# A decoder's expert routing: row numbers by rank replaced by block ids summed on TensorE

## The chip, the cores and the metric

The kernel runs on one core of one Trainium2 chip. Its time is the device time of one execution in microseconds (us). Engines are written PE (TensorE), ACT (ScalarE), DVE (VectorE), POOL (GpSimd) and SP (SyncE, which here only issues DMAs). Each has its own in-order queue of instructions, and they wait for one another through semaphores.

## The reference, cut to what matters

Two decoder layers in float32 on x of shape (16, 64, 128), that is 1024 tokens of width 128, or 8 tiles of 128 tokens. Layer 0: causal self attention with rotary positions (16 heads of width 8), cross attention to `ctx_1024`, then a mixture of 8 experts; layer 1: self attention with 16 heads of width 64, cross attention, then a feed-forward layer with ternary weights. After each of the six a residual sum and a layer norm. The part that the change is about:

```
logits = x_flat @ gate_w.T                      # (1024, 8)
top_v, top_i = top_k(logits, 2)
probs = softmax(top_v)
combine = einsum('tk,tke->et', probs, one_hot(top_i, 8))
for wg, wu, wd, we in experts:                  # wg, wu (512, 128), wd (128, 512)
    hidden = silu(x_flat @ wg.T) * (x_flat @ wu.T)
    acc = acc + we[:, None] * (hidden @ wd.T)
```

## The kernel before, in words

The attention and feed-forward layers run as two streams of tiles, `pre` (self0, cross0: 16 tiles) and `post` (wide, cross1, ternary: 24 tiles). A stream is software pipelined: in step j each engine works for several tiles at different stages (`stream_pe`, `stream_act`, `stream_dve`, `stream_pool`), and hooks (`pre_pe` and its like, lines 1933 to 1982) put other work between. Behind the `pre` stream, the order of what is left of tiles S[5] to S[7] (the last three tiles of cross0), of routing and of the weights' transposes is written out by hand, one list per engine: `drain_pe`, `drain_act`, `drain_dve`, `drain_pool` (lines 1997 to 2097). An engine works through its list strictly in order.

Routing (class `Routed`). The 8 token tiles are taken in groups (`GROUPS`, line 1427: tiles 0-1, 2-3, 4-5, 6, 7). For each group:
- `logits_pe`, `logits_act`: 128x8 logits per tile, copied from PSUM.
- `choose` (DVE): the two best experts by Max8 and its index search, one-hot rows OH, their sum `chosen`, and a running sum `before`.
- `rank_pe`: for each token and expert, the number of earlier tokens that chose it, as products of `chosen` and `before` with constant matrices.
- `place_read`, `place` (DVE): this rank plus the expert's base (1024 rows for each) picked by OH, giving a row number `pos`.
- `scatter` (POOL): two indirect DMAs per tile write the tile's rows into the DRAM tensor `routed` at `pos`, 16 in all. SP has filled `routed` (4544 KB) with zeros before (line 2169).

When all groups are done, `map_dve` works out with 12 small steps which expert each of the 23 blocks of 128 rows belongs to and at which row it starts. `rows_sp` loads 23 starts into SP's registers and loads the blocks of `routed` directly into XG; it stores each block's result back in place. PE and POOL load the 23 expert numbers into registers.

The 24 expert matrices (gate, up, down of 8 experts) come by DMA in natural layout and are turned in place by PE: 4 transposes into one bank and a copy back each (`weights_pe`, `weights_copy`). 17 of them stand in `drain_pe`, the rest at the head of `Routed.pe`; ACT copies 20 and DVE 4 (`DVE_WEIGHTS`).

The block loop (`Routed.pe`, `act`, `dve`, `pool`, lines 1762 to 1866), for block n: transpose of the block's rows (`block_pe`, `block_act`), gate product, Silu on ACT, up product, product of both on DVE (`mul_dve`), down product, copy to YS on DVE (`out_dve`), store. POOL brings the gate and up weights of the block's expert into a ring of three (`bring_pool`, line 1708: a 128x1024 copy from an address in a register), since PE reads them from a fixed place. Between blocks 6 and 12 DVE and POOL also prepare the ternary weights and separate WQKV (three 128x1024 copies, line 1853).

Behind the last block POOL gathers each token's two result rows by `pos` with 16 indirect DMAs (line 1871), DVE weighs and adds them (`combine`), normalises (`rsqrt` on POOL, `apply` on DVE), and the `post` stream starts.

## Time and profile before

| what | us |
|---|---|
| median of 3 runs | 361.52 (359.88 to 361.73) |
| profiled execution, its own time | 356.69 |
| span of the profiled execution | 354.9 |
| PE busy | 315.3 (89% of the span) |
| DVE busy | 226.5 |
| POOL busy | 192.2 |
| ACT busy | 185.1 |

All times of the trace count from the start of the span. A line number such as L1720 is one of the kernel before. A busy PE is not a PE at its peak: its matrix instructions are pipelined and overlap. "Granted clock" is the share of full speed that the chip allowed PE in a stretch: 1.00 is 2.4 GHz, 0.50 is 1.2 GHz. Spans on POOL are rough.

### The profile page before, as it was taken

Reading aid. Unit: us, or ns where it says so; the run is one execution under the profiler, and the core shown is the slowest. Engines: PE = TensorE matmul, PEld = TensorE weight load, DVE = VectorE, ACT = ScalarE, POOL = GpSimd, SP = SyncE. Lnnn points to the kernel's source line nnn. Section 1 sums busy time; section 2 is a strip of 40 time slices with the busy share of each in tenths; the row PEclk is TensorE's granted clock in tenths of the full one; section 3 lists DMA queues with packets and bytes.
Section 4 is the critical chain, followed back from the end, with each engine's and each line's share of the span. In section 5 each row is a group of like instructions: output and inputs, shape, how many; then the busy total and the mean of one; then the engine's idle time right before and its main releaser. Section 6 shows DMA issues by size and latency. Waiting matters only on the chain.

```text
span 354.9 us, 10572 instructions
## 1 busy us (share of the span) xinstructions
PE 315.3 (89%) x4062; PEld 261.5 (74%) x4062; DVE 226.5 (64%) x529; ACT 185.1 (52%) x402; POOL 192.2 (54%) x282
## 2 busy tenths in 40 slices
PE   2769999997896799999995999999999987999993
PEld 2547787886786699999984966688677665887663
DVE  1398988889657334653336475665566675897685
ACT  2276787887466332332223367454435436788641
POOL 2676867885775555534306884231123355486785
PEclk9999999999769999999998799999999999999998
DMA  6899989000111111121011110000000000000001
GB/s 186 233 311 281 293 270 317 12 3 3 39 37 46 53 47 45 46 57 52 22 31 30 46 40 9 2 2 2 2 2 1 4 1 2 2 4 3 3 22 40
DMA packets 35979, 23.04 MB, mean 65 GB/s; under 512 B 4160, under 2 KB 33882, under 8 KB 35802
## 3 DMA queue, kind: packets, MB, share of 16 engines
q1 hardware_dynamic: 34618, 19.64, 19.1%
q0 software_dynamic: 1024, 2.10, 1.9%
q8 instruction: 34, 0.56, 0.7%
q10 hardware_dynamic: 288, 0.62, 0.5%
q14 instruction: 15, 0.12, 0.1%
HBM read 14.60 MB, written 7.73 MB: 63 GB/s over the span
## 4 chain that ended last, share of the span: by engine, by line
PE 70%; DVE 10%; POOL 6%; issue 6%; DMA 3%; ACT 2%; SPq 1%; POOLq 0%; ACTq 0%; DVEq 0%
PE banks L924 9%; PE banks L934 8%; PE banks L1751 6%; PE banks L1720 6%; PE banks L1728 6%; PE banks L463 6%; PE banks L636 5%; PE banks L968 4%; PE banks L609 3%; PE banks L562 2%; PE banks L948 2%; PE banks L1125 2%; PE banks L1493 2%; PE banks L588 2%; PE banks L571 1%
## 5 line engine op out<-in xcount | busy, mean ns | idle before, releaser
L472 ACT ACTIVATE PT<-banks 128x512 f32<-128x512 f32 x64 | 34.8, 597 | 22.2 <-PE banks L463 21.6
L974 ACT ACTIVATE U<-banks 128x512 f32<-128x512 f32 x47 | 28.1, 597 | 28.6 <-PE banks L924 15.3
L1708 POOL COPY U<-WALL 128x1024 f32 x23 | 23.8, 1041 | 33.1 <-PE banks L1728 29.4
L335 POOL TENSOR_SCALAR ve<-mv 128x1 f32<-128x1 f32 x40 | 9.0, 225 | 54.5 <-DVE mv L330 53.8
L1743 DVE TENSOR_TENSOR PT<-banks,PR 128x512 f32<-128x512 f32 x23 | 15.9, 691 | 35.0 <-PE banks L1728 29.0
L451 ACT ACTIVATE PR<-PR 128x1024 f32<-128x1024 f32 x32 | 33.8, 1057 | 6.8 <-DVE PR L445 6.6
L463 PE MATMUL banks<-cst,PR 128*128 128x128 f32 x256 | 34.1, 276 | 2.7 <-issue 0.8
L924 PE MATMUL banks<-XT,WQKV 128*128 128x128 f32 x256 | 33.0, 291 | 0.8 <-ACT XT L1915 0.8
L924 PEld LDWEIGHTS banks<-XT,WQKV 128*128 128x128 f32 x256 | 31.4, 204 | 1.6 <-ACT XT L1915 1.2
L463 PEld LDWEIGHTS banks<-cst,PR 128*128 128x128 f32 x256 | 28.0, 141 | 5.8 <-issue 3.5
L428 DVE TENSOR_REDUCE mx<-banks 128x16 f32<-128x1024 f32 x24 | 29.3, 1220 | 3.8 <-PE banks L620 2.5
L445 DVE TENSOR_TENSOR PR<-banks,mx 128x1024 f32<-128x1024 f32 x24 | 29.4, 1224 | 0.8
L934 PE MATMUL banks<-WALL,XT 128*64 128x512 f32 x128 | 29.2, 598 | 0.0
L780 POOL TENSOR_TENSOR RK<-KQ,cst 128x512 f32<-128x512 f32 x24 | 24.9, 1039 | 4.3 <-DVE KQ L745 2.8
L636 PE MATMUL banks<-VB,PT 128*64 128x18 f32 x768 | 26.3, 212 | 0.0
L1003 POOL TENSOR_TENSOR PR<-PR,rs 128x1024 f32<-128x1024 f32 x8 | 15.2, 1901 | 20.2 <-DVE rs L1013 20.0
L636 PEld LDWEIGHTS banks<-VB,PT 128*64 128x64 f32 x768 | 25.0, 140 | 0.5 <-issue 0.2
L1751 PE MATMUL banks<-WALL,PT 128*128 x184 | 24.4, 276 | 0.6 <-DVE YS L1759 0.6
L1871 POOL DMA_INDIRECT RK<-routed_rows,pos x16 | 15.9, 995 | 16.4 <-DMA routed_rows<-YS 12.3
L337 POOL TENSOR_TENSOR rstd<-ve,half 128x1 f32<-128x1 f32 x40 | 22.7, 568 | 3.3
L1720 PE MATMUL banks<-XGT,U 128*128 128x128 f32 x184 | 24.4, 276 | 0.0
L1728 PE MATMUL banks<-XGT,U 128*128 128x128 f32 x184 | 24.3, 275 | 0.0
(192 smaller groups left out, 711.0 us busy)
## 6 DMA issues: line engine op xcount, KB each, us to landing
routed_rows<-zero SPq DMA_DIRECT2D x1, 4544.0 KB, 19.1
WALL<-in_L_ffn_wg_dram SPq DMA_DIRECT2D x8, 256.0 KB, 5.4
WALL<-in_L_ffn_wu_dram SPq DMA_DIRECT2D x8, 256.0 KB, 5.7
WALL<-in_L_ffn_wd_dram SPq DMA_DIRECT2D x8, 256.0 KB, 6.2
U<-in_L_attn_W_qkv_dram SPq DMA_DIRECT2D x1, 1536.0 KB, 6.7
XG<-routed_rows SPq DMA_DIRECT2D x23, 64.0 KB, 1.8
routed_rows<-YS SPq DMA_DIRECT2D x23, 64.0 KB, 1.6
cst<-shape_constants ACTq DMA_DIRECT2D x1, 537.0 KB, 4.5
```

Source lines behind the costliest of these rows:

```text
L428: dve.tensor_reduce(top_of, s, AX.X, ALU.max).then_inc(self.max.sem, 1)
L445: dve.tensor_tensor(PR[:, n % 2, :].rearrange("q (g h k) -> q g h k", g=4, k=SEQ), s, bc(top_of, 3, SEQ), ALU.subtract).then_inc(self.sub. ...
L451: act.activation(p, p, ACT.Exp, scale=self.scale).then_inc(self.exp.sem, 1)
L463: t = pe.transpose(PS[:, B_PT + m, P * (r % 4):P * (r % 4 + 1)], PR[:, n % 2, P * r:P * (r + 1)], ident)
L472: act.activation(PT[:, n % 2, 4 * m:4 * m + 4, :].rearrange("p r q -> p (r q)"), PS[:, B_PT + m, :], ACT.Copy).then_inc(self.pt.sem, 1)
L636: m = pe.matmul(PS[64 * b:64 * b + 64, B_Y, w * r:w * (r + 1)], PT[:, n % 2, r, 64 * b:64 * b + 64], VB[:, n % 3, r, b].rearrange("p a e - ...
L924: m = pe.matmul(PS[:, bank, P * k:P * (k + 1)], WQKV[:, f // 2, P * u:P * (u + 1)], XT[:, P * i:P * (i + 1)], start=True, stop=True)
L934: m = pe.matmul(PS[64 * a:64 * a + 64, bank, :], XT[:, SEQ * (2 * i + b):SEQ * (2 * i + b + 1)], WVO[:, a, 4 * g:4 * g + 4, :].rearrange(" ...
L974: return eng.activation(o, s, ACT.Copy) if part == 0 else eng.tensor_copy(o, s)
L1720: m = pe.matmul(PS[:, j % 2, P * c:P * (c + 1)], WE[:, j % 3, 0, P * c:P * (c + 1)], XGT[:, j % 3, :], start=True, stop=True)
L1728: m = pe.matmul(PS[:, 2 + j % 2, P * c:P * (c + 1)], WE[:, j % 3, 1, P * c:P * (c + 1)], XGT[:, j % 3, :], start=True, stop=True)
L1751: m = pe.matmul(PS[:, 7, 0:P], HT[:, j % 2, c, :], WALL[:, e, 2, P * c:P * (c + 1)], start=(c == 0), stop=(c == CH - 1))
```

## The change

Routing by ids. `rank_pe` now forms the whole place (base of the expert in blocks, plus rank) from `chosen` of all earlier tiles, so `before` goes; the groups are tiles 0-3, 4-5, 6, 7. `place` splits the place into a block slot (place / 128) and a lane (place mod 128). `mark_lanes` (DVE) writes for each tile and choice a 128x128 one-hot of the lane, `mark_slots` (POOL for tiles 0 to 5, DVE for 6 and 7) a 128x64 one-hot of the slot times the token's number. `ids_pe` sums their products over all tiles in PSUM: a table of token numbers by slot and lane. `go_dve` and `spread_pe` pick from it the 23 used slots, and from the same product comes each block's expert. `ids` are then row numbers for one indirect DMA per block.

SP writes each normalised tile twice into a DRAM tensor in token order (`tokens_sp`); POOL gathers a block's 128 rows by `ids` (`gather`) and scatters a block's result to `results` in token order (`scatter`); SP loads the results directly, one DMA per tile (`results_sp`). The zero fill of 4544 KB becomes one row of 128 values.

The weights of a block are brought by DVE (`bring_dve`) behind `mul_dve`, no longer by POOL. Four of the 24 weight transposes move into steps 6 to 9 of the `pre` stream; choosing, ranking and placing tiles 0 and 1 leaves its last two steps. The four `drain` lists are reordered, all weight copies are ACT's, and the constants come in two DMAs instead of one.

```diff
-        GROUPS = [(0, 2), (2, 4), (4, 6), (6, 7), (7, 8)]
+        GROUPS = [(0, 4), (4, 6), (6, 7), (7, 8)]
+        EARLY_WEIGHTS = 4
+        WEIGHT_BANKS = [B_Y] * EARLY_WEIGHTS + [0, 1, 2] * 3 + [B_Y, B_OX, 0, 1, 2] * 2 + [B_Y]
...
             def rank_pe(self, pe, k):
...
+                pe.wait_ge(*self.sel.at(min(k + 1, LAST)))
                 for t in range(lo, hi):
-                    m = pe.matmul(o, trib[:, :], chosen[:, t, :], start=True, stop=(t == 0))
-                    if t >= 1:
-                        m = pe.matmul(o, onesb[:, :], before[:, t, :], start=False, stop=True)
+                    pe.matmul(o, onesb[:, :], baseb[:, :], start=True, stop=False)
+                    for n in range(t):
+                        pe.matmul(o, onesb[:, :], chosen[:, n, :], start=False, stop=False)
+                    if k < LAST:
+                        m = pe.matmul(o, trib[:, :], chosen[:, t, :], start=False, stop=True)
...
+            def mark_lanes(self, dve, k):
+                dve.wait_ge(*self.places_made(k))
...
+                for t in range(*GROUPS[k]):
+                    for r in range(2):
+                        m = dve.tensor_scalar(LANE[:, t, r, :], cst[:, C_LANE:C_LANE + P], placef[:, t, r, 1:2], None, ALU.is_equal)
+            def mark_slots(self, eng, k, made):
+                eng.wait_ge(*self.places_made(k))
+                for t in range(*GROUPS[k]):
+                    for r in range(2):
+                        m = eng.tensor_scalar(SLOT[:, t, r, :], cst[:, C_LANE:C_LANE + 64], placef[:, t, r, 0:1],
+                                              cst[:, C_TOKEN + 2 * t + r:C_TOKEN + 2 * t + r + 1], ALU.is_equal, ALU.mult)
+            def ids_pe(self, pe, k):
...
+                pe.wait_ge(*self.lanes.at(k + 1))
+                pe.wait_ge(*(self.slots.at(k + 1) if k < 2 else self.late_slots.at(k - 1)))
+                for t in range(lo, hi):
+                    for r in range(2):
+                        m = pe.matmul(PS[0:64, 3, 0:P], SLOT[:, t, r, :], LANE[:, t, r, :],
+                                      start=(t == r == 0), stop=(t == NT - 1 and r == 1))
+            def spread_pe(self, pe):
+                pe.wait_ge(*self.idt.at(1))
+                pe.wait_ge(*self.go.at(3))
+                pe.matmul(PS[:, 3, 256:280], IDT, GO, start=True, stop=True)
+                pe.wait_ge(*self.go.at(4))
+                pe.matmul(PS[0:1, 3, 280:304], WHOSE, GO, start=True, stop=True).then_inc(self.b_mm.sem, 1)
...
+            def tokens_sp(self, sp):
+                for t in range(NT):
+                    sp.wait_ge(*self.prev.ln.at(t + 1))
+                    sp.dma_start(tokens[1:, :].rearrange(by_tile, t=NT, r=2)[t], bc(X[:, t, :], 1, 2)).then_inc(s_tok, 16)
+            def results_sp(self, sp):
+                for k in range(3):
+                    sp.wait_ge(s_ys[k], 16 * len(range(k, BLOCKS, 3)))
+                for t in range(NT):
+                    sp.dma_start(YG[:, t], results[1:1 + 2 * TOKENS, :].rearrange(by_tile, t=NT, r=2)[t]).then_inc(s_yg[t], 16)
+            def gather(self, pool, j):
...
+                if j >= 4:
+                    pool.wait_ge(*self.xt_mm.at(j - 3))
+                pool.indirect_dma_start(XG[:, j % 4, :], None, tokens, bass.IndirectOffsetOnAxis(ids[:, j:j + 1], 0))\
+                    .then_inc(s_xg[j % 4], 16)
+            def scatter(self, pool, j):
+                pool.wait_ge(*self.ycp.at(j + 1))
...
+                pool.indirect_dma_start(results, bass.IndirectOffsetOnAxis(rows[:, j:j + 1], 0), YS[:, j % 3, :], None)\
+                    .then_inc(s_ys[j % 3], 16)
...
             def pe(self, pe):
-                weights_pe(pe, RING, RING + 4)
-                pe.wait_ge(*self.map.at(8))
+                pe.wait_ge(*self.ids.at(2))
                 _, e = nc.values_load_multi_w_load_instructions(
...
-                weights_pe(pe, RING + 4, 3 * EXPERTS)
...
             def dve(self, dve):
+                dve.wait_ge(*self.ids.at(2))
+                _, e = nc.values_load_multi_w_load_instructions(
+                    bi[0:1, 0:3], engines=[mybir.EngineType.DVE], min_val=0, max_val=EXPERTS - 1,
...
+                for j in range(3):
+                    self.bring_dve(dve, j, e[j])
+                _, later_e = nc.values_load_multi_w_load_instructions(
+                    bi[0:1, 3:BLOCKS], engines=[mybir.EngineType.DVE], min_val=0, max_val=EXPERTS - 1,
...
                     if n < BLOCKS:
                         self.mul_dve(dve, n)
+                    if n + 3 < BLOCKS:
+                        self.bring_dve(dve, n + 3, later_e[n])
...
             def pool(self, pool):
+                for j in range(4):
+                    self.gather(pool, j)
+                for n in range(BLOCKS + 1):
+                    if n + 4 < BLOCKS:
+                        self.gather(pool, n + 4)
+                    if n >= 1:
+                        self.scatter(pool, n - 1)
+                    if n in (6, 9, 12):
                         pool.wait_ge(s_wide, 16)
+                        pool.tensor_copy(WQKV[:, n // 3 - 2, :], WRAW[:, n // 3 - 2, :]).then_inc(s_sep, 1)
```

The lists behind the stream, as they are after the change (PE, DVE and POOL; ACT's follows PE's, and ends with the copies of weights 17 to 23, the exponential and the loading of Silu's table):

```
PE:   logits 0, w4, t S7, y S5, va S6, o S5, w5, rank 0, y S6, va S7, o S6, w6, x 4, y S7, w7, x 5, o S7,
      logits 1, w8, ids 0, x 6, w9, rank 1, logits 2, w10, x 7, w11, logits 3, ids 1, w12, rank 2, w13,
      ids 2, rank 3, w14-16, ids 3, w17, spread, w18-23
DVE:  y S5, choose 0, y S6, r S5, ln S4, y S7, r S6, ln S5, place 0, r S7, mark_lanes 0, choose 1, ln S6, ln S7,
      place 1, choose 2, mark_lanes 1, choose 3, place 2, mark_lanes 2, mark_slots 2, place 3, mark_lanes 3,
      mark_slots 3, go, ids
POOL: rsqrt S4, join 0, rsqrt S5, rsqrt S6, rsqrt S7, join 1, mark_slots 0, join 2, mark_slots 1, logit difference
```

## Rows read from the trace of the kernel before

**Rows 1.** The page: shares of the chain that ended last, by engine.

```profile
PE 70%; DVE 10%; POOL 6%; issue 6%; DMA 3%; ACT 2%; SPq 1%; POOLq 0%; ACTq 0%; DVEq 0%
```

**Rows 2.** Stretches: length, busy PE, PEld, DVE, ACT, POOL, clock, DMA.

```profile
98.00:103.00 5.00, 5.00 (x27) 4.66 (x27) 3.37 (x19) 2.54 (x6) 3.33 (x5) 0.50 0.12 39
...
119.40:184.00 64.60, 64.01 (x574) 63.82 (x573) 28.17 (x55) 19.55 (x44) 25.91 (x24) 1.00 0.15 43
...
194.50:290.00 95.50, 92.76 (x1201) 68.42 (x1202) 57.88 (x106) 46.97 (x85) 36.19 (x47) 0.97 0.04 10
```

**Rows 3.** The chain that ended last, in order of time: start, length, work.

```profile
92.80 0.44 PE banks L1493 x4
...
93.24 1.57 PE banks L636 x32
...
113.25 2.19 SPq L1673
...
117.18 1.86 DMA XG<-routed_rows
...
119.41 0.90 PE banks L1720 x8
...
188.36 2.50 DMA RK<-routed_rows,pos
```

**Rows 4.** The timeline at the end of the first stream, DVE.

```profile
81.28 0.23 DVE L1537 MAX8 top<-lg 128x8 f32<-128x8 f32 x2
...
82.59 0.36 DVE L1554 TENSOR_TENSOR before<-before,chosen 128x8 bf16<-128x8 bf16 x2
...
84.12 1.21 DVE L428 TENSOR_REDUCE mx<-banks 128x16 f32<-128x1024 f32 x1
```

**Rows 5.** The timeline behind the stream: DVE, POOL and PE.

```profile
101.27 0.29 DVE L408 TENSOR_TENSOR R<-banks,XR 128x128 f32<-128x128 f32 x1 [0.36 <-PE banks L662]
...
112.30 0.95 POOL L1609 DMA_INDIRECT routed_rows<-X,pos  x1 [0.30 <-DVE bm L1652]
...
114.51 0.53 PEld L1493 LDWEIGHTS banks<-cst,WALL 128*128 128x128 f32 x5 [2.06 <-ACT WALL L1502]
```

**Rows 6.** Groups of POOL instructions: busy, mean ns of one, idle before them.

```profile
L335 POOL TENSOR_SCALAR ve<-mv 128x1 f32<-128x1 f32 x40 | 9.0, 225 | 54.5 <-DVE mv L330 53.8
...
L341 POOL TENSOR_SCALAR X<-R,mv,rstd 128x128 f32<-128x128 f32 x20 | 16.3, 815 | 2.2
...
L1871 POOL DMA_INDIRECT RK<-routed_rows,pos x16 | 15.9, 995 | 16.4 <-DMA routed_rows<-YS 12.3 <-issue 4.1
```

**Rows 7.** Groups of ACT instructions.

```profile
L1502 ACT ACTIVATE WALL<-banks 128x512 f32<-128x512 f32 x20 | 11.4, 598 | 7.1 <-PE banks L1493 6.9
...
L2055 ACT ACT_TABLE_LOAD x1 | 1.3, 1283 | 0.0
```

**Rows 8.** Groups of DVE instructions.

```profile
L1743 DVE TENSOR_TENSOR PT<-banks,PR 128x512 f32<-128x512 f32 x23 | 15.9, 691 | 35.0 <-PE banks L1728 29.0 <-ACT PR L1736 5.9
...
L1759 DVE COPY YS<-banks 128x128 f32<-128x128 f32 x23 | 6.7, 290 | 4.4 <-PE banks L1751 1.6
...
L1069 DVE COPY PT<-lnwb 128x512 f32<-128x512 f32 x1 | 0.4, 415 | 0.0
...
L1086 DVE TENSOR_SCALAR FCT<-FCT,lnwb 128x128 f32<-128x128 f32 x4 | 0.9, 280 | 0.0
```

**Rows 9.** The timeline in block 9, DVE and POOL.

```profile
146.78 3.14 DVE L1058 TENSOR_SCALAR PT<-FCW,gam 128x512 f32<-128x512 f32 x2
...
146.79 1.60 POOL L1853 COPY WQKV<-U 128x1024 f32<-128x1024 f32 x1
```

**Rows 10.** The timeline behind the last block, DVE and POOL.

```profile
189.47 0.86 DVE L1086 TENSOR_SCALAR FCT<-FCT,lnwb 128x128 f32<-128x128 f32 x4
...
189.62 0.95 POOL L1871 DMA_INDIRECT RK<-routed_rows,pos  x1 [0.30 <-issue]
...
190.96 0.35 DVE L1879 SCALAR_TENSOR_TENSOR R<-RK,pk,X 128x128 f32<-128x128 f32 x1 [0.62 <-DMA RK<-routed_rows,pos]
```

More of the change, by code:

```diff
@@ new lines, in place @@
+                dve.wait_ge(*self.chosen_ranks(k))
+                with nc.allow_low_precision(reason="one of eight whole numbers below 8192, the others 0"):
+                    dve.tensor_reduce(rank[:, lo:hi, :], pm[:, 0:n], AX.X, ALU.add).then_inc(self.placed.sem, 1)
+                if k == LAST:
+                    self.count_dve(dve)
+                dve.wait_ge(*self.summed_ranks(k))
+                dve.tensor_scalar(places[:, lo:hi, :, 0], rank[:, lo:hi, :], 7, None, ALU.logical_shift_right).then_inc(self.placed.sem, 1)
@@ L1762, in pe @@
             def pe(self, pe):
-                weights_pe(pe, RING, RING + 4)
-                pe.wait_ge(*self.map.at(8))
+                pe.wait_ge(*self.ids.at(2))
                 _, e = nc.values_load_multi_w_load_instructions(
-                    bi[0:1, 0, 0:BLOCKS], engines=[mybir.EngineType.PE], min_val=0, max_val=EXPERTS - 1,
-                    skip_runtime_bounds_check_because="a sum of seven comparisons, each 0 or 1")
-                weights_pe(pe, RING + 4, 3 * EXPERTS)
+                    bi[0:1, 0:BLOCKS], engines=[mybir.EngineType.PE], min_val=0, max_val=EXPERTS - 1,
+                    skip_runtime_bounds_check_because="the number of one of the eight experts, or 0")
                 self.block_pe(pe, 0)
@@ L1842, in pool @@
             def pool(self, pool):
-                pool.wait_ge(*self.map.at(8))
-                _, e = nc.values_load_multi_w_load_instructions(
-                    bi[0:1, 0, 0:BLOCKS], engines=[mybir.EngineType.Pool], min_val=0, max_val=EXPERTS - 1,
-                    skip_runtime_bounds_check_because="a sum of seven comparisons, each 0 or 1")
-                for s in self.all_copied():
-                    pool.wait_ge(*s)
-                for j in range(BLOCKS):
-                    self.bring_pool(pool, j, e[j])
-                    if j in (6, 9, 12):
-                        pool.wait_ge(s_wide, 16)
-                        pool.tensor_copy(WQKV[:, j // 3 - 2, :], WRAW[:, j // 3 - 2, :]).then_inc(s_sep, 1)
@@ L1930, in decoder_kernel @@
         NB = 4
+        EARLY = {6 + g: g for g in range(EARLY_WEIGHTS)}
         def pre_pe(pe, j, part):
@@ L2055, in drain_act @@
             act.activation(warm[:, 0:1], half[:, :], ACT.Silu)
-            weights_act(act, RING, 3 * EXPERTS)
         def drain_dve(dve):
             a1.y_dve(dve, S[5])
+            moe.choose(dve, 0)
+            a1.y_dve(dve, S[6])
+            a1.r_dve(dve, S[5])
+            a1.ln_dve(dve, S[4])
+            a1.y_dve(dve, S[7])
+            a1.r_dve(dve, S[6])
+            a1.ln_dve(dve, S[5])
+            moe.place(dve, 0)
+            a1.r_dve(dve, S[7])
+            moe.mark_lanes(dve, 0)
@@ L2094, in drain_pool @@
             a1.rsqrt_pool(pool, S[7])
-            for t in range(4, NT):
-                for r in range(2):
-                    moe.scatter(pool, t, r)
+            moe.join_pool(pool, 1)
+            pool.wait_ge(s_cst2, 16)
+            moe.mark_slots(pool, 0, moe.slots)
+            moe.join_pool(pool, 2)
+            moe.mark_slots(pool, 1, moe.slots)
+            pool.wait_ge(*moe.top.at(NT))
+            pool.tensor_tensor(pk[:, 0, :], top[:, :, 1], top[:, :, 0], ALU.subtract).then_inc(moe.diff.sem, 1)
@@ L2168, in _ @@
             sp.wait_ge(s_zt, 1)
[L2169 removed]
+            load(tokens[0:1, :], zero[:, :], s_zr)
             weights.done(sp)
```

573 lines of the change are left out of this document (262 added, 311 removed).

## The prediction, made before the changed kernel was run

> **What bounds the kernel now.** I read the chain that ended last first: PE holds 70% of it [rows 1], so an edit off PE only matters where PE waits. Then the busy time by stage: in the block loop PE is busy 64.01 of 64.60 us at the full granted clock, VectorE 28.17 and GpSimd 25.91 [rows 2], so one of the 23 blocks costs 64.6 / 23 = 2.81 us, all PE. The wide stages behind it are PE too (92.76 of 95.50) [rows 2]. Last, the order of time: between the last tile's value product at 93.24 and the first gate product at 119.41 stand 26 us in which token routing, the turning of the expert weights and the loading of the first block end one after the other, the last links being SP's register loads (2.19 us) and the block's DMA (1.86 us) [rows 3]. In part of this stretch, 98 to 103, PE also ran at a granted clock of 0.50, its 1.2 GHz level [rows 2]. So the change is decided by three places: when the first gate product starts, whether a block stays at 2.81 us, and the way from the last block to the wide stage.
>
> **Part 1, the two streams' end.** Choosing and placing tiles 0 and 1 leaves the stream. Their DVE work stands from 81.28 to 82.95, 1.67 us, and behind it the next row maximum starts at 84.12 [rows 4]; without it the scores would let it start about 1.1 us earlier. Added: four weights turned in steps 6 to 9, each 4 transposes in 0.44 us, as at 92.80 where the clock was still full [rows 3], and a 0.60 us ACT copy [rows 7] in front of the P copies. Steps 6 and 7 have room on PE, 8 and 9 hardly; between 0.4 and 1.8 us, I take 1.2. Net nothing, between -1.8 and +0.7. The zero fill goes: it ran beside the stream, and I price it at nothing; it is cover for no one.
>
> **Part 2, the last tile.** Before, its residual was summed at 101.27 [rows 5], 6.5 us after its value product ended at 94.81, because four weights and two x transposes stood between, at half clock. Now two weights and one x transpose do; with the small DVE steps at 0.18 us each (two took 0.36 [rows 4]) I get its statistics at about 97.6, some 4 us earlier. That is the gain the new order makes.
>
> **Part 3, routing by ids.** What follows is new and serial, since ids_pe(0) stands in PE's queue ahead of x(6), rank(1) and logits(2), and waits for marks that GpSimd can only make after join(1), which waits for choose(1), which VectorE does after mark_lanes(0).
> - 8 lane marks, 128x128, on VectorE: 0.86 / 4 = 0.215 us each as in the scaling of rows 10 (up to the 0.280 of rows 8): 1.7 us, to 99.4.
> - choose(1) 0.95, join on GpSimd 0.3: to 100.7.
> - 8 slot marks, 128x64, on GpSimd, none in the trace: a one-column scalar op takes 0.225, a 128-column one with two scalars 0.815 [rows 6]. By length (0.815 - 0.225) x 64 / 127 + 0.225 = 0.52. 4.2 us, to 104.9; bounds 1.8 and 6.5. PE waits 7 us here, and behind it everything that the later groups need.
> - ids(0) 8 products 0.9, x(6), one weight, rank(1) 1.0, place(1) 1.1, choose(2) 0.7, join 0.3: to 109.1. Four more slot marks 2.1: to 111.2.
> - ids(1), a weight, rank(2) 1.2; place(2) 1.1; marks 0.9: to 114.7. ids(2), rank(3), place(3) with the counting (nine DVE steps of 0.18 to 0.2 and two hops) 2.3; marks and go 1.5; ids(3), copy, spread, ids: 1.0. The block ids stand at 119.5.
>
> Before, the row numbers stood at 113.25 [rows 3]. So in spite of the 4 us won, ids come 6 us later; the block map (12 small DVE steps) that they replace is shorter than two more passes through PE and GpSimd. What waits for them: GpSimd's first indirect gather lands 2.50 us after its start [rows 3], 122.1, not last. PE turns the six weights that stand behind spread, 2.6 us at 0.44, then loads 23 registers, some 1.9 (its idle of 2.06 before line 1493 is that load today [rows 5]): 124. ACT copies seven weights at 0.60 [rows 7], then exp, a table load of 1.28 and a Silu: 125.4, and only then the first block's XT copy, where today the table load lay in PE's gap. VectorE's first three brings wait for the last of those copies, 123.6 to 125.8. First gate product at 125.9, 6.5 us later than 119.41.
>
> **The clock.** This sum has PE at full clock throughout. Today it stood at 0.50 from 98 to 103 though PE was wholly busy there [rows 2]; the way from 93.24 on shows it low too (a value product of 1.57 us), after a stretch with gaps. A 7 us wait makes a fall near 98 to 105 likely: 10 us at half clock adds 1.9 us to the sum, until the block loop 5.8. I take 1.0, between 0 and 5.8: first gate at 126.9, +7.5.
>
> **Part 4, the block loop.** VectorE takes the brings off GpSimd: a 128x512 copy takes 0.415 where the 128x128 ones take 0.215 [rows 8, 10], so 1024 columns some 0.68; bounds 0.6 and the 1.6 of GpSimd's slow copy [rows 9]. With product 0.69 and output 0.29 that is 1.66 of 2.81: no bound, but the FCW work of blocks 6 to 12 has less room. GpSimd now issues two indirect DMAs per block: 0.995 each with 0.30 between [rows 5, 6], 1.26 x 2 = 2.52 of 2.81 us. It has 0.3 us to spare per block, and between blocks 6 and 12 three 1.60 us copies [rows 9], 4.8 + 0.6 for their hops. A gather is issued 1.9 us ahead of need; the first copy fits into that, the second and third push PE back, as 0.3 us a block pays back only 0.9 between them: 1.8 x 3 - 1.9 - 6 x 0.2 = 2.3. I take +2.5, between 0 and +5.
>
> **Part 5, behind the last block.** The last scatter (2.5 to landing) and direct loads (about 2.0) replace a direct store and two gathers: by their own count the first combine could start 1.6 us sooner than 190.96. But in VectorE's queue the four scalings ahead of it end at 190.33 [rows 10]: -0.6. The 16 gathers leave GpSimd in the first wide tiles, where PE is 97% busy: at most the 2.7 idle of 95.5 [rows 2], I take -0.6.
>
> **Sum.** 7.5 + 2.5 - 0.6 - 0.6 = 8.8, rounded to 8.5 since I rounded waits up. The profiled execution took 356.69 (span 354.9); by it, 365.2. The runs shown have a median of 361.52, 4.8 above it; on that scale 370.0. A difference under 0.5%, 1.8 us, can't be told from none.
>
> **A rule against the change.** At 146.78 two VectorE scalar ops took 3.14 us, beside GpSimd copies, against 0.415 for a like-sized copy: the two engines do exclude one another there [rows 8, 9]. But a GpSimd indirect DMA beside four VectorE scalings took 0.95, no more than its mean of 0.995 [rows 6, 10], so the sum has no lock between a bring and a gather. The Trainium skill's page SBUF - State Buffer, section SBUF: two separate sides, says otherwise: while VectorE runs a copy in a two-port mode, descriptors of a DMA issued from GpSimd can't be written. By that rule the block loop would stretch as in the second rival.
>
> **Rivals.**
> - **The marks are cheap and the clock stays up (faster), 0.10.** Slot marks at 0.225 take 3.6 off, the early weights hide wholly (-1.2), the copies fit into the loop (-2.5), and with PE fed from the ids on, the clock no longer falls at the wide stage's head: 0.97 over 95.5 us [rows 2] is 2.9 us. 8.5 - 3.6 - 1.2 - 2.5 - 2.9 - 1.0 = -2.7: 358.8. For it: both falls follow PE gaps. Against it: ids_pe(0) is a new gap. It decides once a slot mark costs under 0.3 us.
> - **VectorE's brings hold up GpSimd's DMAs, 0.15.** GpSimd's block work becomes 2.52 + 0.68 = 3.20, above PE's 2.81: 23 x 0.4 = 9.0 more, since the copies then have no slack at all: 379. For it the 3.14 us, against it the 0.95.
> - **No difference, 0.07.** Marks at their floor and the copies fitting, the clock as now: 8.5 - 3.6 - 1.2 - 2.5 = +1.2: 362.7, within 1.8 of before.
> - **The ids hide behind the weights, 0.08.** PE turns weights too slowly at 1.2 GHz for the routing to matter; the 4 us won in part 2 then come through, less the register load and the table load: about +3, 364.5.
> - **The routing chain as summed, 0.60:** 370.0, its own range 365 to 376.
>
> **Numbers.** Slower by over 0.5%: 0.60 + 0.15 + 0.08 = 0.83; same 0.07; faster 0.10. The range goes from the ids-hidden case's lower side, 362.5, to the lock's 379: left out are the faster case and half of the no-difference one below, and a low clock on top of the lock above.
>
> **What would show it.** PE idle some 7 us ahead of the first id product, ended by GpSimd's slot marks; ids copied near 119 to 122; the first gate at 124 to 130; a block period of 2.8 outside blocks 6 to 14, with PE waiting for XG in them; DMA_INDIRECT at 0.95 to 1.0 beside the brings (1.6 and more if the lock holds); first combine 6 to 7 us after the last down product. I am wrong if slot marks take under 0.3 us, if the last tile's statistics are not near 98, or if the loop period is above 2.9 throughout.

## The result, and the profile of the changed kernel

Before: 360.7 us median of four runs beside the changed kernel. Changed: 376.23 us (374.48 to 380.92). The ratio is 1.042 [1.034, 1.050], slower, by 15.5 us where 8.5 were forecast. Medians are of all executions, while ratios, here and below, leave out those that took over 1.5% more than the fastest of the same kernel, so a ratio need not be that of the medians beside it. The profiled execution took 375.29 against 356.69; that is 18.6, since the one of before lay 4.0 under its median and the one of after 0.9. The ledger is in profiled time:

| stretch, by TensorE's rows | before | after | change | forecast |
|---|---|---|---|---|
| to the transposes of P, last stream step | 88.65 | 91.98 | +3.3 | 0 |
| from there to the first gate product | 30.6 | 40.2 | +9.6 | +7.5 |
| from there to the last down product | 64.9 | 69.8 | +4.9 | +2.5 |
| from there to the wide stage's first product | 10.4 | 10.5 | +0.1 | -0.6 |
| from there to the end | 160.4 | 160.9 | +0.5 | -0.6 |

The page's chain of the changed kernel, and its stretches (columns as in [rows 2]):

```profile
PE 65%; POOL 10%; issue 7%; DVE 7%; DMA 6%; ACT 2%; SPq 0%; POOLq 0%; DVEq 0%; ACTq 0%
```

```profile
92.00:107.00 15.00, 8.04 (x119) 6.78 (x117) 8.64 (x52) 5.30 (x13) 7.17 (x16) 0.90 0.13 36
107.00:132.20 25.20, 18.48 (x145) 15.91 (x145) 9.23 (x48) 11.03 (x24) 6.79 (x11) 0.79 0.02 6
132.20:202.30 70.10, 67.05 (x578) 64.93 (x578) 41.57 (x82) 17.98 (x45) 48.40 (x45) 1.00 0.16 41
```

Against [rows 1], PE fell from 70 to 65% of the chain, and GpSimd rose from 6 to 10, DMA from 3 to 6. In the block loop the clock is full and PE has the same work, but GpSimd went from 25.91 [rows 2] to 48.40 us.

**The stretch behind the stream**, from the timeline (start, length, work, and in brackets idle time and what ended it):

```profile
99.92 1.64 DVE L1604 TENSOR_SCALAR RK<-cst,placef 128x128 f32<-128x128 f32 x8
102.73 4.54 POOL L1612 TENSOR_SCALAR U<-cst,placef 128x64 f32<-128x64 f32 x8
107.42 3.59 PE L1625 MATMUL banks<-RK,U 128*64 128x128 f32 x16 [7.09 <-POOL U L1612]
112.12 0.19 DVE L1584 TENSOR_TENSOR pm<-OH,banks 128x32 f32<-128x32 bf16 x1 [9.06 <-PE banks L1565]
113.90 2.47 POOL L1612 TENSOR_SCALAR U<-cst,placef 128x64 f32<-128x64 f32 x4
116.51 1.06 PE L1625 MATMUL banks<-RK,U 128*64 128x128 f32 x8 [2.54 <-POOL U L1612]
120.72 1.08 PE L1625 MATMUL banks<-RK,U 128*64 128x128 f32 x4 [1.05 <-DVE U L1612]
126.50 0.18 DVE L1646 CAST ids<-banks 128x24 uint32<-128x24 f32 x1 [0.54 <-PE banks L1639]
130.28 2.02 DVE L1746 COPY U<-WALL 128x1024 f32 x3 [3.52 <-ACT WALL L1497]
132.19 1.13 PE L1758 MATMUL banks<-XGT,U 128*128 128x128 f32 x8
```

TensorE waits three times for marks, twice for GpSimd's and once for VectorE's: 7.09, 2.54 and 1.05 us, 10.7 together. VectorE then waits 9.06 for TensorE: the ranks of group 1 stood behind the first id products.

**The block loop**, blocks 7 to 10, and two rows further on:

```profile
151.68 1.14 POOL L1717 DMA_INDIRECT XG<-token_rows,ids  x1 [0.30 <-issue]
152.02 0.68 DVE L1746 COPY U<-WALL 128x1024 f32 x1
153.18 0.98 POOL L1724 DMA_INDIRECT expert_rows<-YS,rows  x1 [0.36 <-DVE YS L1797]
154.16 1.60 POOL L1898 COPY WQKV<-U 128x1024 f32<-128x1024 f32 x1
154.81 1.52 DVE L1746 COPY U<-WALL 128x1024 f32 x1
155.93 1.27 POOL L1717 DMA_INDIRECT XG<-token_rows,ids  x1 [0.17 <-issue]
157.50 1.07 POOL L1724 DMA_INDIRECT expert_rows<-YS,rows  x1 [0.30 <-issue]
158.88 0.97 POOL L1717 DMA_INDIRECT XG<-token_rows,ids  x1 [0.31 <-issue]
162.35 0.33 PE L1733 MATMUL banks<-cst,XG 128*128 128x128 f32 x1 [0.48 <-DMA XG<-token_rows,ids]
176.74 0.68 DVE L1746 COPY U<-WALL 128x1024 f32 x1
176.92 1.36 POOL L1724 DMA_INDIRECT expert_rows<-YS,rows  x1 [0.30 <-issue]
```

Up to the copy GpSimd's round has TensorE's period, 2.79 us, because it waits for it: the 0.36 ahead of the scatter is a wait for VectorE's output. With the 0.30 that stand between any two issues in its place, GpSimd's own work is 0.30 + 1.14 + 0.30 + 0.98 = 2.72 us, so 0.07 is spare. The 1.60 us copy goes nearly whole into lateness. Behind it GpSimd issues back to back, and a round takes 2.57 where the gather meets no bring (158.88 to the next one's start at 161.45), which pays back 0.2. The 1.14 is a wait as well: the gather's issue ends 0.12 after VectorE's bring does (152.82 and 152.70). In nine issues of the loop the distance is 0.11 or 0.12 us, and the scatter that was issued 0.18 behind the start of a bring took 1.36.

**Behind the last block** the first combine starts 7.07 us after the last down product, against 6.9 before [rows 10] (190.96 less 184.1):

```profile
202.86 0.97 POOL L1724 DMA_INDIRECT expert_rows<-YS,rows  x1 [0.78 <-DVE YS L1797]
209.07 0.35 DVE L1908 SCALAR_TENSOR_TENSOR R<-RK,pk,X 128x128 f32<-128x128 f32 x1 [0.81 <-DMA RK<-expert_rows]
```

### The profile page after: what moved, and what is told of

Its sections match the earlier page's. It is cut to its first block, busy times and chain, and to the rows that moved or that the text cites. A ratio compares the mean times of both kernels' runs of the same rounds, so it can differ in the third digit from the quotient of the medians.

```text
span 373.4 us, 10661 instructions
## 1 busy us (share of the span) xinstructions
PE 325.7 (87%) x4136; PEld 267.6 (72%) x4136; DVE 237.6 (64%) x550; ACT 185.1 (50%) x406; POOL 193.2 (52%) x289
## 4 chain that ended last, share of the span: by engine, by line
PE 65%; POOL 10%; issue 7%; DVE 7%; DMA 6%; ACT 2%; SPq 0%; POOLq 0%; DVEq 0%; ACTq 0%
PE banks L939 9%; PE banks L949 8%; PE banks L478 6%; PE banks L651 5%; DMA XG<-token_rows,ids 4%; PE banks L983 3%; PE banks L1789 3%; PE banks L624 3%; PE banks L1766 3%; PE banks L1758 3%; PE banks L577 2%; POOL XG L1717 2%; PE banks L1492 2%; PE banks L603 2%; POOL expert_rows L1724 2%
## 5 line engine op out<-in xcount | busy, mean ns | idle before, releaser
L1774 ACT ACTIVATE PR<-banks 128x512 f32<-128x512 f32 x23 | 13.7, 597 | 47.9 <-PE banks L1758 47.9
L478 PE MATMUL banks<-cst,PR 128*128 128x128 f32 x256 | 34.7, 280 | 1.9 <-issue 0.8
L1717 POOL DMA_INDIRECT XG<-token_rows,ids x23 | 25.1, 1093 | 17.4 <-DVE bi L1647 11.1
L478 PEld LDWEIGHTS banks<-cst,PR 128*128 128x128 f32 x256 | 28.8, 143 | 4.6 <-issue 2.8
L1724 POOL DMA_INDIRECT expert_rows<-YS,rows x23 | 23.2, 1007 | 16.9 <-DVE YS L1797 13.5
L462 DVE TENSOR_TENSOR PR<-banks,mx 128x1024 f32<-128x1024 f32 x24 | 29.4, 1224 | 0.8
L1758 PE MATMUL banks<-XGT,U 128*128 128x128 f32 x184 | 24.4, 275 | 0.0
```

The costliest lines, as they stand in the source:

```text
L462: dve.tensor_tensor(PR[:, n % 2, :].rearrange("q (g h k) -> q g h k", g=4, k=SEQ), s, bc(top_of, 3, SEQ), ALU.subtract).then_inc(self.sub. ...
L478: t = pe.transpose(PS[:, B_PT + m, P * (r % 4):P * (r % 4 + 1)], PR[:, n % 2, P * r:P * (r + 1)], ident)
L1717: pool.indirect_dma_start(XG[:, j % 4, :], None, tokens, bass.IndirectOffsetOnAxis(ids[:, j:j + 1], 0))\
L1724: pool.indirect_dma_start(results, bass.IndirectOffsetOnAxis(rows[:, j:j + 1], 0), YS[:, j % 3, :], None)\
L1758: m = pe.matmul(PS[:, j % 2, P * c:P * (c + 1)], WE[:, j % 3, 0, P * c:P * (c + 1)], XGT[:, j % 3, :], start=True, stop=True)
```

## The experiments

All times are medians; ratios are to the kernel before, which ran beside each. "Distance" is from TensorE's transposes of P in the last stream step to its first gate product: 30.6 us before, 40.2 changed. The stream moves with the clock (step 5 began between 31.1 and 33.6 us in profiles with the same code up to there), so I compare distances rather than times of day.

### The id products behind the last ranks

```
             weights_pe(pe, 8, 9)
-            moe.ids_pe(pe, 0)
             moe.x_pe(pe, 6)
...
             moe.logits_pe(pe, 3)
-            moe.ids_pe(pe, 1)
             weights_pe(pe, 12, 13)
...
-            moe.ids_pe(pe, 2)
             moe.rank_pe(pe, 3)
+            moe.ids_pe(pe, 0)
+            moe.ids_pe(pe, 1)
+            moe.ids_pe(pe, 2)
             weights_pe(pe, 14, 17)
```

> The changed kernel with one edit: on TensorE the id products of groups 0, 1 and 2 stand behind the rank products of group 3, the last, so that nothing of the drain queues behind the marks. Theory (the queue): in the changed kernel TensorE stood 7.09 us ahead of its first id product, until POOL's last slot mark of group 0 at 107.4, and everything behind it (the logits and ranks of groups 1 to 3) came late by that. Without it the ids should be copied some 6 to 7 us earlier (126.5 less 6.5, 120), the first gate product should start at 124.5 to 127 instead of 132.2, and the time should fall by 5 to 7, to about 370. Rival (the work): POOL's and VectorE's marks themselves are what is late; POOL's slot marks of group 1 ended at 116.5 and those of groups 2 and 3 follow VectorE's choices, so the first gate product moves by under 2 us and the time stays at 374 to 376, only with the idle time of TensorE lying further back.

Measured: 368.41 us, ratio 1.019 [1.007, 1.032]. Timeline and stretch:

```profile
106.37 4.63 POOL L1612 TENSOR_SCALAR U<-cst,placef 128x64 f32<-128x64 f32 x8
108.12 0.19 DVE L1584 TENSOR_TENSOR pm<-OH,banks 128x32 f32<-128x32 bf16 x1 [1.42 <-PE banks L1565]
112.86 3.27 PE L1625 MATMUL banks<-RK,U 128*64 128x128 f32 x28
124.94 1.57 PE L1758 MATMUL banks<-XGT,U 128*128 128x128 f32 x8
```

```profile
92.00:107.00 15.00, 13.37 (x118) 11.96 (x117) 8.26 (x44) 5.08 (x14) 3.53 (x9) 0.50 0.07 19
```

The queue it was. The marks cost what they did (4.63), 3.6 us later in the day because here TensorE ran at 0.50 from 92 to 107, and still the ids and the first gate product came 7.3 us earlier: the ranks of group 1 no longer wait for the marks of group 0, and all 28 id products run in one go of 3.27 us. Distance 33.7, although the changed kernel's 40.2 were run at a clock of 0.90; the comparison at like clock stands with the four edits below.

### The early weights out of the stream

```
-        EARLY_WEIGHTS = 4
+        EARLY_WEIGHTS = 0
...
             moe.logits_pe(pe, 0)
-            weights_pe(pe, 4, 5)
+            weights_pe(pe, 0, 1)
...
             moe.logits_pe(pe, 1)
-            weights_pe(pe, 8, 9)
+            weights_pe(pe, 4, 9)
             moe.ids_pe(pe, 0)
```

> The changed kernel with the four early weight pairs taken out of steps 6 to 9 of the stream and put at the places in the drain of the four that came first there; four more stand ahead of the first id product, where TensorE waited 7.09 us. Theory (the early weights cost what they take from the stream, and the drain has room): in the changed kernel the stream's steps came out 3.3 us later from step 6 to step 9 than before; without the weights statistics of step 7 should come 2 to 3 us earlier (about 96.5 instead of 99.2 on VectorE), the idle time ahead of the first id product should shrink by about 2, and the time should fall by 2 to 3, to 373 to 374. Rival (they were free: the steps were late for the three constant casts on VectorE or for the clock): no earlier statistics, and four weight pairs more in the drain cost up to 1.5, so 376 to 378.

Measured: 374.50 us, ratio 1.047 [1.040, 1.054]. First the changed kernel at steps 5, 7 and 9, then this one at steps 5 and 9 (timeline, TensorE; P's transposes are L478's):

```profile
33.02 1.06 PE L478 MATMUL banks<-cst,PR 128*128 128x128 f32 x8 [0.80 <-issue]
43.31 0.66 PE L1492 MATMUL banks<-cst,WALL 128*128 128x128 f32 x4 [0.83 <-ACT VB L732]
54.19 1.04 PE L478 MATMUL banks<-cst,PR 128*128 128x128 f32 x8
```

```profile
32.47 1.06 PE L478 MATMUL banks<-cst,PR 128*128 128x128 f32 x8 [0.80 <-issue]
50.88 1.04 PE L478 MATMUL banks<-cst,PR 128*128 128x128 f32 x8
```

From step 5 to step 9 it is 18.4 us instead of 21.2; the kernel before took 17.9. The four weights cost 2.8, not the 1.2 I had. TensorE's wait ahead of the first id product shrank to 5.27 us. The stream ended 2.9 earlier (89.10 against 91.98), the first gate product came at 130.3, 1.9 earlier, and the time fell by 1.7, and the ratio is no better than the changed kernel's: between the two sets of runs this can't be told.

### WQKV's copies on ScalarE

```
-                    if n in (6, 9, 12):
-                        pool.wait_ge(s_wide, 16)
-                        pool.tensor_copy(WQKV[:, n // 3 - 2, :], WRAW[:, n // 3 - 2, :]).then_inc(s_sep, 1)
...
                         self.block_act(act, n + 2)
+                    if n in (6, 9, 12):
+                        act.wait_ge(s_wide, 16)
+                        act.activation(WQKV[:, n // 3 - 2, :], WRAW[:, n // 3 - 2, :], ACT.Copy).then_inc(s_sep, 1)
```

> The changed kernel with the three copies of WQKV in blocks 6, 9 and 12 moved from POOL to ScalarE, nothing else. In the changed kernel the block loop took 69.85 us (first gate product to last down product) against 64.65 before. Theory (POOL was full: gather, scatter and these copies filled its queue from 153 to 190, and each copy stretched a bring of weights on VectorE to 1.5 to 2.6 us from 0.68): without the copies the loop should take 65 to 66.5, the brings all 0.6 to 0.8 us, and the time fall by 3.5 to 5, to 371 to 373. Rival (the brings alone hold back POOL's descriptors, and the rows of the experts' inputs land late whatever the copies do): the loop stays at 68 to 70, and the time within 1.5 of 376.

Measured: 375.18 us, ratio 1.047 [1.041, 1.053]. Group and loop stretch:

```profile
L1746 DVE COPY U<-WALL 128x1024 f32 x23 | 15.7, 689 | 3.5 <-ACT WALL L1497 3.5
```

```profile
136.20:202.80 66.60, 66.01 (x578) 65.62 (x578) 37.41 (x81) 22.12 (x48) 43.99 (x42) 0.98 0.17 43
```

The loop fell by 3.5 us, to 66.6, with TensorE busy for all but 0.6 of it, and the brings at 0.689 instead of 0.872 on average. So this part of the theory stands. But the time did not fall: the profiled execution ran from 92 to 111 at a granted clock of 0.50, where the changed kernel's had 0.82 (0.90 up to 107), and its first gate product came at 136.2, 4 us later, with no edit up to there. The four runs had granted clocks of 0.935 to 0.954, those of the changed kernel 0.945 to 0.973. Why it draws the lower clock more often stays open; the gain is seen when the queue ahead of it is mended too (below).

### The brings cut to two columns

```
+                if j < 3:
                     dve.tensor_copy(WE[:, j % 3].rearrange("p w i -> p (w i)"),
...
+                else:
+                    dve.tensor_copy(WE[:, j % 3, 0, 0:2], WALL[:, e, 0, 0:2]).then_inc(self.we.sem, 1)
```

> The changed kernel with the bring of block weights cut from the 256 columns to 2 for all blocks from the fourth on, so those blocks multiply with old weights: the rest of each expert's weights is left out. The copies of WQKV stay on POOL. It separates the brings' own effect on POOL's indirect DMAs from that of the WQKV copies. Theory (the brings cost little by themselves, 0.15 us for each indirect DMA they meet, and the copies fill POOL's queue): indirect DMAs at 0.97 to 1.0 us everywhere, loop 2 to 3 us shorter than 69.85, that is 67 to 68, with waits for the gathered rows still there at blocks 10 to 16. Rival (brings are what makes the loop long): loop back at 64.6 to 65.5 with the copies still on POOL.

This kernel leaves out the rest of each expert's gate and up weights from the fourth block on. Measured: one run, 374.71 us. Loop stretch, group, and timeline around the second copy and at the third:

```profile
134.30:202.70 68.40, 66.00 (x578) 64.67 (x578) 32.22 (x81) 17.82 (x45) 45.91 (x45) 1.00 0.16 42
```

```profile
L1717 POOL DMA_INDIRECT XG<-token_rows,ids x23 | 23.2, 1007 | 17.4 <-DVE bi L1647 11.1 <-issue 5.8 <-PE banks L1733 0.5
```

```profile
163.03 0.16 DVE L1750 COPY U<-WALL 128x2 f32 x1
163.19 0.97 POOL L1717 DMA_INDIRECT XG<-token_rows,ids  x1 [0.30 <-issue]
165.46 1.59 POOL L1901 COPY WQKV<-U 128x1024 f32<-128x1024 f32 x1
165.82 1.28 DVE L1750 COPY U<-WALL 128x2 f32 x1
173.74 0.98 POOL L1724 DMA_INDIRECT expert_rows<-YS,rows  x1 [0.30 <-issue]
174.53 1.81 DVE L1750 COPY U<-WALL 128x2 f32 x1
174.73 1.56 POOL L1901 COPY WQKV<-U 128x1024 f32<-128x1024 f32 x1
```

The loop took 68.4 against 70.1: without the brings 1.7 are saved, where 2 to 3 were expected, and without the WQKV copies 3.5. From the third block's gate product to the last one's, which leaves out the differing heads of the loops, it is 55.8 us before, 59.6 changed, 57.5 here and 55.9 with the copies on ScalarE. So the brings alone cost nothing in the time of the loop, the copies alone 1.7, and both together 3.8. A gather is issued in 0.97 without a bring and 1.14 beside one. In the run with the copies on ScalarE, too, its issue ends 0.12 to 0.13 after the bring in 15 of the blocks. And a two-column VectorE copy of 0.16 us took 1.28 when it began 0.36 after GpSimd's copy: it ended with that (165.82 + 1.28 = 167.10; 165.46 + 1.59 = 167.05). It waited for the other engine; it did not share with it. The one at 174.53 began 0.20 before GpSimd's copy, while the scatter was being issued, and was held to that copy's end as well (176.34 and 176.29). A two-column copy that began late in a scatter's issue, with no GpSimd copy behind it, ended with the issue (171.74 + 0.30 = 172.04; 171.09 + 0.98 = 172.07), so an issue holds VectorE's copies too.

### Slot marks of groups 0 and 1 on VectorE

```
             moe.mark_lanes(dve, 0)
+            dve.wait_ge(s_cst2, 16)
+            moe.mark_slots(dve, 0, moe.slots)
...
             moe.mark_lanes(dve, 1)
+            moe.mark_slots(dve, 1, moe.slots)
...
-            moe.mark_slots(pool, 0, moe.slots)
             moe.join_pool(pool, 2)
-            moe.mark_slots(pool, 1, moe.slots)
```

> The changed kernel with the slot marks of groups 0 and 1 on VectorE right behind the lane marks instead of on POOL, the id products where they are. On POOL the eight of group 0 took 4.54 us (0.57 each) and TensorE waited for the last; on VectorE those of groups 2 and 3 took 0.31 each. Theory (the engine of the marks is what is late): eight marks in 2.5 us from about 101.6, TensorE's wait of 7.1 us ahead of the id products shrinks to 4 to 5, the first gate product moves by 2 to 3.5 us to 129 to 130, and the time to 373 to 374. Rival (the marks now stand ahead of the choices of group 1 on VectorE and delay these by 2.5 us, and the later groups set the ids' end): first gate product within 1 us of 132, or later than it.

Measured: 373.70 us, ratio 1.030 [1.021, 1.039]. Timeline:

```profile
103.59 1.87 DVE L1612 TENSOR_SCALAR U<-cst,placef 128x64 f32<-128x64 f32 x8
105.61 3.39 PE L1625 MATMUL banks<-RK,U 128*64 128x128 f32 x16 [3.19 <-DVE U L1612]
```

The marks took 1.87 instead of 4.54, TensorE's wait 3.19 instead of 7.09, and the distance fell to 35.3, by 4.9. The theory holds, and more comes than it said, since the later groups' marks gain too. Placing the products later is worth more than making the marks faster (10.8 of distance at like clock, see the two edits below, against 4.9).

### The three casts out of the stream

```
-            if j == 6 and part == 2:
-                dve.wait_ge(s_cst2, 16)
-                dve.tensor_copy(onesb[:, :], cst[:, C_ONES:C_ONES + P]).then_inc(s_rt, 1)
...
             moe.choose(dve, 0)
+            dve.wait_ge(s_cst2, 16)
+            dve.tensor_copy(onesb[:, :], cst[:, C_ONES:C_ONES + P]).then_inc(s_rt, 1)
...
```

> The changed kernel with only the three constant casts on VectorE moved from step 6 of the stream to behind the first choice of the drain. With the early weights out of steps 6 to 9 these steps took 18.4 us against 17.9 before, which leaves 0.5 for the casts. Theory: the transposes of step 9 start 0.4 to 0.7 us earlier by the distance from those of step 5 (that is 20.5 to 20.8 us instead of 21.2) and nothing is lost in the drain, where TensorE waits 7 us. Rival (the casts lie in idle time of VectorE): the distance stays at 21.2.

Measured: one run, 377.53 us, from which nothing can be read at this size. From step 5 to step 9 the trace has 20.7 us (31.86 to 52.59) instead of 21.2: the casts cost 0.4 to 0.5 there, as expected, and the distance stays (40.1).

### The two, and the four edits together

> The changed kernel with two edits together: the id products of groups 0 to 2 behind the last rank product, and the three copies of WQKV on ScalarE. Alone, the first brought the first gate product from 132.2 to 124.9 us, the second the block loop from 69.8 to 66.3 us (with its first 20 us at a granted clock of 0.93, which is over 1 us of it). Theory (two separate losses that add): first gate product at 123 to 126, loop 64.8 to 66.5, time 375 to 376 less 7 less 4, that is 363.5 to 366.5, a ratio to the kernel before of 1.010 to 1.018. Rival (one bottleneck seen twice, POOL's queue from the marks to the last gather): an earlier start only makes the gathers wait elsewhere, and the time stays at 368 to 370, a ratio of 1.02 to 1.03.

Measured: 362.99 us, ratio 1.010 [1.006, 1.014]. Then all four:

> The two edits of the run before, and two more: the four early weight pairs in the drain instead of stream steps 6 to 9, and the three constant casts behind the first choice instead of in stream step 6. The early weights out of the stream brought its end from 91.3 to 89.1 us, and the casts should bring 0.5. Theory (nothing of the change but its longer chain from the places to the ids is left): stream's end 88.5 to 89, first gate product 121.5 to 124, loop 64.8 to 66.5, time 361.5 to 364.5, a ratio of 1.004 to 1.012: the kernel before is still ahead by the marks and ids, which it did not have. Rival (TensorE has no room in the drain once the id products no longer hold it up, so four weight pairs there cost as much as in the stream, 2.2 us): within 0.7 us of the run with two edits.

Measured: 358.74 us, ratio 0.996 [0.993, 1.000]. The gate products' row (min, median and max ns, first and last start) of the changed kernel, the one with two edits and the one with four; then two rows of the last one's timeline:

```profile
L1758 PE MATMUL banks<-XGT,U x184: 275/275/346, 132.2 to 198.5; 128*128 128x128 f32 x184
```

```profile
L1758 PE MATMUL banks<-XGT,U x184: 275/275/455, 120.6 to 183.6; 128*128 128x128 f32 x184
```

```profile
L1758 PE MATMUL banks<-XGT,U x184: 275/275/436, 117.7 to 180.8; 128*128 128x128 f32 x184
```

```profile
104.26 0.17 PE L1561 MATMUL banks<-baseb,onesb 128*128 128x8 bf16 x1 [1.56 <-POOL chosen L1536]
105.49 3.27 PE L1625 MATMUL banks<-RK,U 128*64 128x128 f32 x28
```

The separate losses add: distances 29.4 and 30.3, loops from first to last gate product 63.0 and 63.1 against 66.3 changed and 61.3 before. Of the 15.5 us nothing is left; four edits of place and the same arithmetic give a kernel whose time is between the same and 0.7% shorter than before. The rival of both runs falls, and with four edits the first gate product (117.7) and the time came 3 to 4 us below the lower ends of what I expected. From step 5 to step 9 it is 17.9 us again, as before.

Distances must be read with the clock of their stretch:

| kernel | granted clock, 92 to 107 us | distance, us |
|---|---|---|
| before | 0.66 | 30.6 |
| changed | 0.90 | 40.2 |
| the WQKV copies on ScalarE (same code up to the loop) | 0.50 | 44.9 |
| id products last | 0.50 | 33.7 |
| id products last, WQKV copies on ScalarE | 0.89 | 29.4 |
| the four edits | 1.00 | 30.3 |

At like clock the order in TensorE's queue is worth 10.8 us (0.90 and 0.89) and 11.2 us (0.50 and 0.50), more than the 7.3 in the time of day. What the new chain costs against the old one at like clock no pair shows: before ran at 0.66, the mended ones at 0.89 to 1.00, or at 0.50. The loops' remaining 1.8 sits at their head, where the first gate products ran at the slow rate (maxima of 455 and 436 ns against 275; the granted clock was 0.50 from 117.4 to 120 in the run with four edits); from there the chain of the kernel with four edits has a gate group every 2.79 (124.18, 126.97, 129.75).

### The joined choices, and ScalarE's table load

```
             moe.choose(dve, 2)
+            moe.join_pool(dve, 2)
...
             moe.mark_slots(pool, 0, moe.slots)
-            moe.join_pool(pool, 2)
             moe.mark_slots(pool, 1, moe.slots)
```

> The kernel with four edits and one more: the joined choices of group 2 are added on VectorE right behind its choices instead of on POOL, where they stood behind eight slot marks. In the run with four edits TensorE waited 1.56 us for them, until POOL began at 103.96 us. Theory (an instruction of 0.2 us queued behind 4.6 us of marks still holds TensorE): rank products of group 2 at about 102.6 to 103 instead of 104.26, first gate product 0.8 to 1.6 us earlier (by its distance from the transposes of the last stream step, 30.3 us, down to 28.7 to 29.5), time 357 to 358. Rival (the id products wait for POOL's marks of group 0 anyway, which end at 103.96, and those of group 1 at 106.2): the distance falls by 0.5 at most and the time stays within 0.5 of the run with four edits.

Measured: 358.67 us, ratio 0.999 [0.995, 1.003]. Timeline:

```profile
102.63 0.17 PE L1561 MATMUL banks<-baseb,onesb 128*128 128x8 bf16 x1
104.39 1.96 PE L1625 MATMUL banks<-RK,U 128*64 128x128 f32 x16
106.65 0.62 PE L1625 MATMUL banks<-RK,U 128*64 128x128 f32 x4 [0.30 <-POOL U L1612]
```

The ranks came at 102.63 as the theory had it, and the distance is 29.5, by 0.8 shorter; now the marks of group 1 end last. In the times it does not show.

Then, in addition, on ScalarE:

```
-            weights_act(act, 12, 17)
+            weights_act(act, 12, 14)
+            act.wait_ge(*moe.diff.at(1))
+            act.activation(pk[:, 1, :], pk[:, 0, :], ACT.Exp).then_inc(moe.e2.sem, 1)
+            act.activation(warm[:, 0:1], half[:, :], ACT.Silu)
+            weights_act(act, 14, 17)
             moe.ids_act(act)
...
```

> The same, and ScalarE's Exp of the mixing weights with the table load for Silu (1.28 us) stands ahead of its last ten weight copies, in a stretch where it was idle for 3.65 us, instead of behind them: in the run with four edits it lay between the last weight copy (115.5) and the copy of the first gathered block (117.12), whose rows had landed at 115.75. Theory (what is left ahead of the first gate product is ScalarE's trail): distance from the last stream step to the first gate product down by another 1.0 to 1.5 us against the run with the join alone, time 355.5 to 357, a ratio to the kernel before of 0.985 to 0.992. Rival (the rows or VectorE's bring of the first block's weights, which needs the last weight copy and takes 0.68, come last then): the distance falls by 0.3 to 0.8, and the time by no more than 0.5.

Measured: 359.06 us, ratio 0.999 [0.995, 1.002]. The profiled execution had a granted clock of 0.56 from 92 to 107, so its distance (33.8) can't be set beside those at full clock; from the first gather's start to the first gate product it is 4.26 us (117.61 to 121.87), against 4.69 (112.36 to 117.05) without the edit:

```profile
120.76 0.28 ACT L1739 ACTIVATE XGT<-banks 128x128 f32<-128x128 f32 x1 [0.61 <-PE banks L1733]
121.70 0.33 PE L1733 MATMUL banks<-cst,XG 128*128 128x128 f32 x1 [0.98 <-DMA XG<-token_rows,ids]
```

The rival holds: with the table load gone the first block's transposed input was there at 121.04, but TensorE's queue has the second block's transposition ahead of the first gate product, and its rows landed at 121.70. 0.4 us gained, not 1.0 to 1.5.

## Why the prediction was half right

**The mechanism and its place were right.** "ids_pe(0) stands in PE's queue ahead of x(6), rank(1) and logits(2)", a wait of 7 us (7.09), slot marks of 4.2 (4.54), lane marks of 1.7 (1.64), and three losses in the order forecast. The time lies in the range, but only since the rival with the lock had stretched it to 379: the main case's own range ended at 376, 0.2 below the median. Of its signs, the ids (126.5, not 119 to 122), the first gate product (132.2, not 124 to 130) and the issue of a gather beside a bring (1.14, not 0.95 to 1.0) missed. The sum had half of what came, by four terms:

- **Part 1, net 0: measured +3.3.** The early weights cost 2.8, not 1.2 (bounds 0.4 to 1.8, so the bound failed too): against the run without them each of the steps 6 to 9 grew by 0.5 to 1.0 us, where a pair's transposes keep PE for 0.6 ahead of P's and one also waited 0.83 for ScalarE. No step had room. I had left the three casts out: 0.5. The choices' leaving gave back 1.6 (1.1 said). The other 1.7 arose ahead of step 5, in code that the change does not touch: from 14 to 25 us PE ran slowly (its sixteen score products at 19.2 took 1.16 instead of 0.69, P's eight transposes at 21.9 took 1.91 instead of 1.09), though the profile has the granted clock at 1.00 there in both kernels. What slowed it stays open.
- **Part 2** held: the last tile's statistics stood at 100.0, less the 3.3 of part 1 that is 96.7, against 97.6.
- **Part 3, +6.5, and 1.0 for the clock: measured +9.6.** The step that failed is ids(0), "8 products 0.9". The trace has two for each of the eight, and they ran at half clock (0.52 from 107.4 to 111): 3.59, where sixteen take 1.96 at the full clock (104.39 in the run with the join). So 1.1 of the miss is the count and 1.6 the clock. The ranks of group 1 stand behind them. From 107 to 132.2 the granted clock was 0.79, the way from group to group was costed at full clock, and each of its hops came late; ids at 126.5, less the 3.3 of part 1 that is 3.7 after my 119.5. The clock's 1.0 was too low, within its bounds. From ids to gate 5.7 instead of 7.4 (the clock's 1.0 is in it) gave some back.
- **Part 4, +2.5: measured +4.9.** I counted 2.52 of 2.81 for two indirect DMAs and so 0.3 to spare; 0.995 and 0.30, twice, is already 2.59. A gather beside a bring takes 1.14, the round's work 2.72, and 0.07 is spare. The three copies, 4.8 us long, then cost 3.8 from the third block on. The other 1.2 is at the head, where my sum had nothing: the first two gate groups followed after 2.99 and 2.92 instead of 1.90 and 2.79, with TensorE waiting 0.81 for gathered rows at 134.1. The bring of 0.68 was right.
- **Part 5, -0.6 and -0.6: measured +0.1 and +0.5.** I said the scalings would end last ahead of the first combine; the scatter took 3.8 us to land after its start at 202.86 and the load behind it came last. Why the wide stage and what follows took 0.5 more and not 0.6 less is not shown.

**The rule against the change was right, and only the price that my rival gave it was wrong.** I took the 0.95 of one indirect DMA beside four VectorE scalings for "no lock". That row could not tell: the scalings ended at 190.33 and the issue at 190.57, so an issue held until 0.12 after them would have taken 0.95 as well. Here the bring ends late enough to show it. It costs a gather 0.17 us, not the 0.68 of my second rival, since 0.3 of the issue were done when the bring began, but it takes most of the slack that the loop had; and between a VectorE copy and a GpSimd copy the lock is whole: 0.16 became 1.28. The Trainium skill, page SBUF - State Buffer, section SBUF: two separate sides, calls the shared ports an exclusive lock that whichever starts first holds for its whole instruction. The two-column copy at 165.82 agrees, and so does the one at 174.53, if the scatter then being issued had the ports. That page of the Trainium skill, in the same section, has the descriptors of a GpSimd DMA shut out while such a copy runs. The trace agrees: the issue ended 0.12 us after the bring.

**What no text of mine had seen** is that most of the loss was not in what the change computes. Ids summed on PE are serial, as I argued, but with the products behind the last ranks the first gate product stands as far behind the stream as before (29.4 to 30.3 against 30.6, the latter at a lower clock). My sum took the order in the queue as part of the routing's price; it was a choice of place. What decides TensorE's clock between 92 and 107 us (0.50 to 0.56 in three profiles of the changed kernel and its variants, 0.84 to 1.00 in the others, with no edit that goes with it) stays open; it is worth some 4 us either way.

## What to carry to other kernels

A product that needs marks from two other engines goes in TensorE's queue behind everything that these engines still need from TensorE; early in the queue it makes its own inputs' successors late (10.8 us here at like clock). Before giving an engine one more job per round, sum its round with the durations that it has beside its new neighbours, not with its mean alone: 2.52 of 2.81 became 2.72 of 2.79, and odd jobs of 4.8 us in that queue then cost 3.8. A clock that differs from profile to profile can hide a gain (the loop's 3.5 us did not show in the time of its own run, whose granted clock was lower ahead of the loop), so judge an edit by the stretch that it changes, beside a profile with a like clock there, and the time by all of the edits together.

## What was not expected of the hardware

- A VectorE copy that begins during a GpSimd copy waits for its end, whatever its own size: 128x2 took 1.28 us instead of 0.16, 128x1024 brings took 1.52 and 1.65 instead of 0.68. Two that began 0.20 and 0.44 us before GpSimd's copy, while an indirect DMA was being issued, were held as well: 1.81 for 128x2, 2.59 for a bring.
- GpSimd's indirect DMA is issued in 0.97 us alone. With a 128x1024 VectorE copy of 0.68 that begins 0.2 to 0.5 us into it, the issue ends 0.12 us after the copy (1.14 in most rounds); issued 0.18 behind the copy's start it took 1.36.
- A marking op of 128x64 with two column scalars takes 0.57 us on GpSimd and 0.23 on VectorE (8 in 4.54 and in 1.87).
- The same code up to 92 us ran the next 15 us at a granted clock of 0.50 in one profile and 0.90 in another, with the first gate product 4 us later.
- TensorE's products can run at a slow rate where the profile has the granted clock at 1.00: 1.16 us for sixteen score products instead of 0.69, from 14 to 25 us of the changed kernel.
